# A batched attention with additive bias: how the row maximum reaches the query rows, how far ahead it is taken, and how the last value product is laid over the column groups

## The reference, cut to what matters

```python
q = (query @ Wq.T + bq).reshape(B, T, H, D).transpose(0, 2, 1, 3)      # B=8, T=256, H=16, D=8
k = (key @ Wk.T + bk).reshape(B, S, H, D).transpose(0, 2, 1, 3)        # S=1601
v = (value @ Wv.T + bv).reshape(B, S, H, D).transpose(0, 2, 1, 3)
scores = jnp.einsum('bhtd,bhsd->bhts', q, k) * scale + attn_mask       # attn_mask is T x S
scores = jnp.where(pad, -jnp.inf, scores)
probs = jax.nn.softmax(scores, axis=-1)
out = jnp.einsum('bhts,bhsd->bhtd', probs, v)
```

## Time and profile before

| | us |
|---|---|
| median of 3 runs | 3205.91 (3191.13 to 3212.24) |
| the profiled execution, its own time | 3200.54 |
| its span in the profile | 3198.4 |
| first forward matmul of the first attention | at 170.7 |
| first `cover` | at 188.2 |
| last value product of it | about 929.7 |
| mean TensorE clock over the span | 0.933 of full |

### The profile page before, as it was taken

How to read it: one execution, slowest core, us unless ns; L and a number is a source line. 1 busy time by engine, 2 the same in 40 slices (tenths; PEclk the granted TensorE clock), 3 DMA queues, 4 the chain that set the end, 5 groups by cost and what they waited for, 6 DMA issues and landing times. The chain is left out here.

```text
span 3198.4 us, 81679 instructions
## 1 busy us (share of the span) xinstructions
PE 2822.6 (88%) x31874; PEld 1626.7 (51%) x31874; DVE 2005.7 (63%) x6463; ACT 1442.7 (45%) x2237; POOL 1341.4 (42%) x1205
## 2 busy tenths in 40 slices
PE   4579999999993593899999999999999999994998
PEld 3423333333353472566666666666666666663544
DVE  3467777777745435767676666766666667644443
ACT  2236666666640132454544545445455464441111
POOL 2000000000000002688787887878878788781000
PEclk8779999999985795999999999999999999996999
DMA  5511111111100002000000000000000000001000
GB/s 148 169 42 20 23 20 20 22 20 23 23 4 26 1 0 90 7 7 24 7 17 12 7 24 5 19 12 7 22 7 19 12 7 7 7 2 45 0 0 13
DMA packets 91811, 75.04 MB, mean 23 GB/s; under 512 B 25745, under 2 KB 83801, under 8 KB 90942
## 3 DMA queue, kind: packets, MB, share of 16 engines
q1 hardware_dynamic: 91454, 70.08, 8.5%
HBM read 56.69 MB, written 13.49 MB: 22 GB/s over the span
## 5 line engine op out<-in xcount | busy, mean ns | idle before, releaser
L1448 ACT ACTIVATE a_probs<-psS 128x1024 f32<-128x1024 f32 (+1 forms) x448 | 431.3, 963 | 632.0 <-PE psS L1329 628.0
L633 ACT ACTIVATE a_probs<-psS 128x1024 f32<-128x1024 f32 (+2 forms) x512 | 440.2, 866 | 299.1 <-PE psS L579 282.2
L1765 POOL TENSOR_TENSOR a_acc<-a_acc,a_probs 128x512 f32<-128x512 f32 x320 | 407.1, 1272 | 228.3 <-ACT a_probs L1448 225.5
L1771 POOL MEMSET a_shut<- 128x3328 f16 x1 | 2.9, 2871 | 1175.9 <-POOLq L1130 1175.9
L1352 PE MATMUL psX<-a_probs,a_values 128*64 128x256 f32 x3328 | 446.2, 386 | 1.7 <-issue 0.2
L660 DVE CUSTOM_DVE_ANT_0 a_junk<-psT,a_mask 128x384 f16<-128x384 f32 (+1 forms) x683 | 377.2, 573 | 109.3 <-PE psT L555 58.2
L1767 POOL TENSOR_TENSOR a_acc<-a_acc,a_probs 128x512 f32<-128x512 f32 x320 | 406.7, 1271 | 25.1
L1609 DVE CUSTOM_DVE_ANT_0 a_junk<-psT,a_mask 128x400 f16<-128x400 f32 (+1 forms) x514 | 282.3, 572 | 155.0 <-PE psS L1304 87.0
L1609 DVE CUSTOM_DVE_ANT_0 a_junk<-psS,a_mask 128x400 f16<-128x400 f32 (+1 forms) x510 | 280.5, 572 | 151.5 <-PE psT L1304 87.5
L590 PE MATMUL psX<-a_probs,a_values 128*9 128x256 f32 x3328 | 295.9, 385 | 3.2 <-issue 2.2
L1352 PEld LDWEIGHTS psX<-a_probs,a_values 128*64 128x64 f32 x3328 | 224.5, 137 | 105.5 <-issue 24.3
(11 more groups left out here) (315 smaller groups left out, 5703.5 us busy)
## 6 DMA issues: line engine op xcount, KB each, us to landing
a_kd<-p_kst SPq DMA_DIRECT2D x24, 416.0 KB, 3.2
a_wq<-in_wq SPq DMA_DIRECT2D x64, 128.0 KB, 2.0
a_keys<-a_kd SPq DMA_DIRECT2D x96, 75.0 KB
p_ctx<-in_ctx SPq DMA_DIRECT2D x8, 768.0 KB
a_ctx<-in_ctx SPq DMA_DIRECT2D x8, 768.0 KB
a_queries<-a_md SPq DMA_DIRECT2D x256, 0.5 KB
p_mask_raw<-in_mask_t SPq DMA_DIRECT2D x16, 224.0 KB, 4.5
a_queries<-a_qd SPq DMA_DIRECT2D x64, 52.0 KB
```

Of the source, the lines that this page charges most:

```text
L633: nc.scalar.activation(dst, src, ACT.Exp).then_inc(exp_done, 1)
L1448: nc.scalar.activation(dst, src, ACT.Exp).then_inc(exp_done, 1)
L1765: nc.gpsimd.tensor_tensor(acc, acc, src[:, :, 0, :], ALU.add).then_inc(sum_step, 1)
```

## The change

Three edits. First, `store_max`, `md` and `max_out` are gone; `give_max` sends `lowest` straight from SBUF into row `MAX_ROW`, 128 pieces of 2 fp16 numbers (4 bytes) into one row of 512 bytes, twice. Second, `AHEAD0` is 2 in place of 4. Third, the product of the thirteenth chunk, 256 tokens in column group 0, becomes four products of 64 tokens, one in each column group. (The words "values of a head in three runs" describe what `weigh` did and does: behind the covers of slots 1, 2 and 3. No line of the diff alters it.)

```diff
-        w.md = nc.dram_tensor("a0_md", (4, T), F16, kind="Internal").ap()
...
-        AHEAD0 = 4
+        AHEAD0 = 2
...
-                def store_max(n):
-                    sp.wait_ge(max_done, n + 1)
-                    if n >= 2:
-                        sp.wait_ge(max_out[n % 2], 16 * (n // 2))
-                    if n >= 4:
-                        sp.wait_ge(max_stored[n % 2], 32 * (n // 2 - 1))
-                    sp.dma_start(w.md[n % 4].rearrange("(p t) -> p t", t=TT), lowest[:, n % 4, :]).then_inc(max_out[n % 2], 16)
-
                 def give_max(n):
                     buf, hh = place(n)
-                    sp.wait_ge(max_out[n % 2], 16 * (n // 2 + 1))
+                    sp.wait_ge(max_done, n + 1)
                     if n >= 2:
                         sp.wait_ge(max_stored[n % 2], 32 * (n // 2))
                     for p0 in (0, 64):
                         r = p0 + MAX_ROW
-                        sp.dma_start(queries[r:r + 1, buf, hh, :], w.md[n % 4:n % 4 + 1, :]).then_inc(max_stored[n % 2], 16)
+                        sp.dma_start(queries[r:r + 1, buf, hh, :].rearrange("o (p t) -> o p t", t=TT),
+                                     lowest[:, n % 4:n % 4 + 1, :]).then_inc(max_stored[n % 2], 16)
...
                     if 0 <= it + AHEAD0 < HEADS:
-                        store_max(it + AHEAD0)
-                    if 0 <= it + AHEAD0 - 1 < HEADS:
-                        give_max(it + AHEAD0 - 1)
+                        give_max(it + AHEAD0)
...
-                    for at in range(SLOT_START[sl], SLOT_START[sl] + len(SLOT_ORDER[sl])):
+                    for at in range(SLOT_START[sl], min(SLOT_START[sl] + len(SLOT_ORDER[sl]), SC - 1)):
                         o = 32 * (at % 4)
                         ins = nc.tensor.matmul(psO[o:o + VW, :], w.values[:, b, PROB_ORDER[at], h, :],
                                                probs[:, n % 2, at, :], start=(at < 4), stop=False, skip_group_check=True)
                     if sl == 3:
+                        for j in range(4):
+                            t = slice(64 * j, 64 * j + 64)
+                            ins = nc.tensor.matmul(psO[32 * j:32 * j + VW, t], w.values[:, b, PROB_ORDER[SC - 1], h, :],
+                                                   probs[:, n % 2, SC - 1, t], start=False, stop=False,
+                                                   skip_group_check=True)
                         ins.then_inc(pv_done, 1)
...
                     if n >= 4:
-                        dve.wait_ge(max_out[n % 2], 16 * (n // 2 - 1))
+                        dve.wait_ge(max_stored[n % 2], 32 * (n // 2 - 1))
```

More of the change, by code:

```diff
@@ L479, in attend0 @@
         s.sem(f"a0_{n}") for n in ("const_loaded", "mask_loaded", "cleared", "clamped"))
-    max_out = [s.sem(f"a0_max_out{i}") for i in range(2)]
     max_stored = [s.sem(f"a0_max_stored{i}") for i in range(2)]
```

## The result

The changed kernel takes 3113.45 us as the median of 4 runs (3107.01 to 3119.45), against 3206.71 (3191.13 to 3212.24) for the kernel before in 4 runs: a ratio of 0.9716, 95% interval 0.9677 to 0.9756, or 93 us less. The forecast was 40 us less (3166), with a range that ended at 3145. The sign was right, the forecast size was less than half of what came.

The account below looks back on a forecast made before the run. PE's own stream was taken to bound the loop, at 5.34 us per head. On the profiled 3200.54 us, 35 off for the split and 5 for the lead-in gave 3160.5, as a median 3166; range 3145 to 3215.

Parts of the forecast that it names:

- 44 us of disturbances: Loop over the heads: time beyond the clean pace, some 44 us, left as it was with 10 us either way.
- Part one: Thirteenth chunk's value product in slot 3: splitting it saves 0.27 us per head, 35 us in all, bounds 24 and 40.
- the head shrinks and the loop does not: Loop over the heads: the sign that the forecast is wrong, meaning that the stops grew; no size given.
- Part two: Lead-in ahead of the loop: two iterations of lead instead of four save 5 us, between 3 and 6.6.
- rival D: Slot 3 and loop start: split gives only its lower bound, clock rises late; 27 us saved, 3179 us; chance 0.11.
- Part three: The maximum's way to slot 0's score: sent directly it costs 0, with 4.07 us of margin to land.
- Never released by the DMA of `a_lowest`: Scores of slot 0: the expected sign that PE never waits for the maximum's DMA; no size given.
- B: Score of slot 0: the maximum comes late in every head, giving 3230 or 3454 us; chance 0.14.
- C: Score of slot 0: maximum late only behind a load of keys, once in four heads, 38 us, giving 3204; chance 0.17.
- Rows 8 against rows 4 agree: The maximum's DMAs: store to DRAM up to 8.1 us, read into SBUF 3.3, taken to fit slow DRAM write receipts.

Follow-up runs that it names:

- l4_copy4: The changed kernel with a lead of four iterations and an unread store per head of 128 packed 4-byte pieces to DRAM: 3289.17 us, ratio 1.0243.
- pad64: The kernel before with the maximum stored to DRAM in 128 padded pieces of 64 bytes and read back as 4 of every 64: 3157.88 us, ratio 0.9833.
- split_only: The kernel before with only the thirteenth chunk's product split over the four column groups: 3183.35 us, ratio 0.9968.
- lead4: The changed kernel with `AHEAD0 = 4`, so the kernel before with the direct maximum and the split: 3114.94 us, ratio 0.9755.
- l4_spread4: The changed kernel with a lead of four and an unread DRAM store per head of 128 4-byte pieces, 64 bytes apart: 3118.43 us, ratio 0.9716.
- copy4: The changed kernel, lead of two, with the old store of 128 packed 4-byte pieces to DRAM added, unread: 3364.81 us, ratio 1.0543.
- l4_copy64: The changed kernel with a lead of four and an unread DRAM store per head of 128 pieces of 64 bytes: 3116.77 us, ratio 0.9698.

## Why the prediction was wrong, point by point

- **The step that failed** is the treatment of the 44 us of disturbances, "that the change has no plain handle on", as a term of nothing: "I leave them as they are, with 10 us either way", and, for the way of the maximum, "No gain is bought, as PE does not wait for it now: the best end is 0". The change had the handle: `store_max` caused them (the unread store of l4_copy4 brings them back, the padded one of pad64 removes them from the kernel before). They were 42.7 us in the profiled loop of before and are 2.0 in that of after, four times the 10 us that the range allowed for. The signs stood in the rows that the prediction had read: a store of 512 bytes that took up to 8.1 us while loads of as many pieces took 2.1 to 4.6, SP waiting 246 us for it, and a stretch of half clock. It took them for the price of a wait that nobody on PE shares. A DMA so slow is a sign that something else is held up, and the right question was which.
- **Part one** was mis-sized by a tenth: 0.30 us per head in place of 0.27, 38 us against 35, within 24 to 40. The split product costs 0.96 - 0.30 - 0.55 = 0.11 us, the lower bound (0.105), not 0.15. So "the second round's load cannot start before the first is in place" cost nothing: those loads are hidden too. The estimate by the rule of the Trainium skill that the prediction cites, 0.157, was too high as well. In the trace the eight loads begin at 244.79, 0.22 us ahead of their first matmul (245.01).
- That split_only gained 10 us and not 38 was foreseen in one sentence ("the head shrinks and the loop does not, which would mean that the stops grew"), and was the case without the other edit.
- **Part two**, 5 us (3 to 6.6), came out about right. From lead4 to after, first forward to first cover went from 187.1 - 169.6 = 17.5 us to 182.3 - 173.2 = 9.1, 8.4 gained (predicted 8.3); the 127 heads took 655.1 in place of 651.1, 4.0 lost. Net 4.4 in the traces, and nothing that the medians can show. The 4.0 are three things. The last three of the 127 heads carry forward work that they don't have in lead4: 14.9 us in place of 13.5, 1.4 lost (predicted 1.7). The first two take 12.0 in place of 10.0, 2.0 lost: the loop began at 182.3 but ran at half clock until 191.5, in lead4 from 187.1 until 190.5. This is what rival D had of the clock, at 2.0 in place of up to 3.6. The 0.6 that is left lies between. With the 44.8 us of disturbances, the 127 heads add up: 38.1 + 44.8 - 4.0 = 78.9, and 78.8 were measured. Windows of the changed kernel:

```profile
182.30:191.50 9.20, 9.20 (x90) 2.51 (x89) 6.65 (x28) 4.48 (x5) 0.00 (x0) 0.50 0.09 15
182.30:194.40 12.10, 12.10 (x147) 3.55 (x146) 8.80 (x36) 6.41 (x8) 0.00 (x0) 0.62 0.14 34
191.50:200.00 8.50, 8.50 (x151) 3.18 (x147) 7.04 (x28) 6.18 (x9) 0.00 (x0) 1.00 0.14 40
```

  and of lead4:

```profile
187.10:197.10 10.00, 9.88 (x139) 3.35 (x138) 8.66 (x34) 6.24 (x8) 0.00 (x0) 0.83 0.11 23
```

- **Part three's margin** held. Predicted were 4.07 us between reduction and score, 3.6 of them for the second DMA. The two DMAs are issued in 1.11 us together, not in 0.34 each and a gap (246.98 above), and land after 2.0 us in the median. The page of the changed kernel, part 6:

```profile
a_queries<-a_lowest SPq DMA_DIRECT2D x256, 0.5 KB, 2.0
```

  From the reduction's end (246.95) that is 0.03 + 0.56 + 2.0 = 2.6 of the 4.07, and the maximum was late a few times only, in the waits over 182.3 to 845:

```profile
PEld psS L568 <- DMA a_queries<-a_lowest: 4.5, 12, 0.7
...
PE psS L568 <- DMA a_queries<-a_lowest: 1.1, 3, 0.4
```

  "Never released by the DMA of `a_lowest`" was too strong, and the 5.6 us are an upper limit: PE's and PEld's waits overlap, and a gap of 0.23 stands there in a clean head too, put down to "issue" (254.37 in the earlier trace rows). **B** did not come, and **C** neither: six of the twelve rows have just that 0.23, and the twelve don't follow the loads, which come once in four heads, but stand partly three heads apart. What sets those few was not looked for.
- **D** was wrong on the product and half right on the clock.
- "Rows 8 against rows 4 agree", said of the Trainium skill's sentence that the write receipt is slowest when DRAM is the target, doesn't hold: the 8.1 us of the earlier trace rows come from the packing. The same 4-byte pieces of `lowest` land in 1.7 us in DRAM when spread (l4_spread4) and in 2.0 us in one row of SBUF.

## What to carry to other kernels

Don't write a DRAM buffer in small packed pieces from many partitions in a loop. 128 pieces of 4 bytes side by side cost 43 to 142 us here per 128 stores without PE, DVE or ACT waiting for the data; with the pieces 64 bytes apart, padded to 64 bytes, or sent to SBUF directly they cost nothing that the traces show. When a clean pattern explains less than the whole of a loop, the rest is a term of its own: look for the DMA that lands slower than its kin, and ask whether the change touches it, before calling it noise. And an edit that saves work on PE should be judged with such stops removed: the same split took 16.8 us off the 127 heads with them and 38 to 40 without.

## What the runs showed of the hardware that was not expected

- A packed store of 4-byte pieces to DRAM stops engines that don't use the data: all of PE, DVE and ACT stood for about 3 us, by the modelled ends with inputs ready (before, PE from 210.6 and all three until 213.4), and the releaser is not on the core's engines. In the same kernels the blocks of code take 3.1 us (before) or 3.8 (l4_copy4) to load in place of 1.1. Slow code loading goes with the stops in every run, but it isn't needed for one: in the stop of before that ends at 268.3 no block of code was loading, and the kernel's own DMAs moved 0.10 MB from 264.0 to 268.4. That both are victims of the store's packed writes fits this, but isn't shown. Why completed work is not signalled for 3 us stays open.
- The clock falls to 0.50 behind a stop (before, 6.8 us at 212.7, with PE idle from 210.6 to 214.1, and four more of 3.4 us each); l4_copy4 has a mean of 0.93 and copy4 0.90. In all kernels without the packed store it is at half in the lead-in, rises between 188 and 198 us, and stays at full to the loop's end.
- 128 pieces of 4 bytes packed into one SBUF row do no such harm: two such DMAs per head are in every kernel with the direct maximum, they land in 2.0 us, and the loop is clean.
- The issue of such a DMA into one row takes SP's queue about 0.55 us each (1.11 for two). That of a store of 128 pieces to DRAM took 0.34 in the median in before and pad64, where it is the first DMA behind SP's wait for DVE, and 0.59 in l4_copy4, l4_copy64 and l4_spread4, where it stands behind the two. It went with the place in SP's order, not with the size or the packing of the pieces.
